# Walking the attention scores by head group instead of by query tile, with the last block's schedule moved 32 slots later

## What is computed

```
x = x + 0.5 * ffn(layernorm(x))          # "b" in the kernel
x = x + attention(layernorm(x))          # 16 heads of 16 features, top 31 of 512 keys kept
x = x + 0.5 * ffn(layernorm(x))          # "a" in the kernel

attention: Q, K, V = x W^T + b;  scores = Q K^T / 4
           thresh = 31st largest of each row of 512 scores; smaller ones become -inf
           softmax, times V, heads joined, times Wo^T + bo
ffn:       rw = softmax over 16 experts of gated cosine logits (at least 2 experts)
           q, k, v = sum over experts of rw * (h W_e);  causal attention over the 512 tokens, 64 wide
           output = sum over experts of rw * (attn o_proj_e)
```

## Time and profile before

| what | value |
|---|---|
| median of 3 runs | 4930.05 us (4927.84 to 4933.91) |
| the profiled execution | 4933.91 us, of which the span from first to last instruction is 4932.1 us |
| busy share of the span | DVE 92%, PE 82%, POOL 75%, ACT 69%, PEld 67% |
| mean granted TensorE clock | 0.915 of full speed |
| DMA | mean 47 GB/s, queue 1 busy 16.5% of 16 engines |

### The profile page before, as it was taken

The page is one execution under the profiler, slowest core; times in us unless marked ns, Lnnn a source line. Parts: engine busy times, 40 slices in busy tenths (PEclk is TensorE's granted clock), DMA queues, the critical chain, the costliest instruction groups (busy, mean ns, idle before and its releaser), DMA issues.

```text
span 4932.1 us, 111636 instructions
## 1 busy us (share of the span) xinstructions
PE 4021.6 (82%) x29004; PEld 3308.1 (67%) x29004; DVE 4550.9 (92%) x10838; ACT 3383.9 (69%) x8261; POOL 3711.1 (75%) x5070
## 2 busy tenths in 40 slices
PE   5767888888888888888888988888888888877667
PEld 4555766776777667676776767777677677765556
DVE  0199999999999999999999999999999999999990
ACT  2366777777777777777777777777777777766662
POOL 4456788878878787878878787888878788865554
PEclk8887999999999999999999999999999999998778
DMA  2201111111111111111111111111111111111011
GB/s 83 51 20 33 47 50 49 52 48 47 53 46 53 48 51 48 51 50 49 51 46 53 48 50 48 49 51 48 51 48 53 47 52 48 50 38 27 20 28 49
DMA packets 243181, 232.19 MB, mean 47 GB/s; under 512 B 27075, under 2 KB 176580, under 8 KB 242244
## 3 DMA queue, kind: packets, MB, share of 16 engines
q1 hardware_dynamic: 242500, 224.49, 16.5%
HBM read 214.98 MB, written 9.44 MB: 46 GB/s over the span
## 4 chain that ended last, share of the span: by engine, by line
issue 37%; POOL 30%; PE 17%; DVE 10%; ACT 3%; DVEq 1%; POOLq 1%; SPq 1%; ACTq 0%; DMA 0%
POOL HS L899 13%; DVE M L802 6%; PE pQ L490 6%; POOL S L940 6%; POOL mixT L917 4%; DVE W L804 3%; PE pFa L434 2%; PE pFa L438 2%; PE pST L474 1%; PE pST L507 1%; PE pFb L458 1%; PE pFa L378 1%; PE pO L531 1%; DVEq L240 1%; PE pFa L380 1%
## 5 line engine op out<-in xcount | busy, mean ns | idle before, releaser
L490 PE MATMUL pQ<-wf_sb,HS 128*128 128x192 f32 x8192 | 1679.8, 366 | 475.0 <-POOL HS L899 473.7
L802 DVE MAX8 M<-W 128x8 f32<-128x512 f32 x3072 | 1953.4, 675 | 0.0
L490 PEld LDWEIGHTS pQ<-wf_sb,HS 128*128 128x128 f32 x8192 | 1545.1, 216 | 556.5 <-POOL HS L899 431.3
L804 DVE MATCH_REPLACE8 W<-M,W 128x512 f32<-128x512 f32 x2048 | 1363.0, 670 | 0.0
L940 POOL TENSOR_TENSOR S<-S,RL 128x512 f32<-128x512 f32 x1024 | 1306.4, 1277 | 0.0
L706 ACT ACTIVATE RL<-S,NBI 128x512 f32<-128x512 f32 x1024 | 762.4, 745 | 388.9 <-POOL S L940 387.4
L935 POOL TENSOR_TENSOR NBI<-M,edge 128x4 f32<-128x4 f32 x512 | 102.1, 199 | 881.1 <-DVE M L802 850.7
L711 ACT ACTIVATE S<-S,NBI 128x512 f32<-128x512 f32 x1024 | 748.4, 731 | 2.1 <-POOL S L940 2.1
L695 ACT COPY S<-pST 128x512 f32<-128x512 f32 x1024 | 525.2, 600 | 242.7 <-PE pST L474 242.7
L804 DVE MATCH_REPLACE8 W<-M,S 128x512 f32<-128x512 f32 x1024 | 681.5, 670 | 0.0
L802 DVE MAX8 M<-S 128x8 f32<-128x512 f32 x1024 | 648.6, 672 | 29.5 <-issue 28.7
(11 more groups left out here) (219 smaller groups left out, 5477.9 us busy)
## 6 DMA issues: line engine op xcount, KB each, us to landing
RB<-rows_b SPq DMA_DIRECT2D x384, 256.0 KB, 3.2
RB<-rows_a SPq DMA_DIRECT2D x384, 256.0 KB, 3.3
x_b<-in_x SPq DMA_DIRECT2D x64, 128.0 KB, 2.8
out_y<-y SPq DMA_DIRECT2D x64, 128.0 KB, 1.7
wf_sb<-in_wf SPq DMA_DIRECT2D x1, 3072.0 KB, 10.4
wof_sb<-in_wof SPq DMA_DIRECT2D x1, 1024.0 KB, 12.4
rows_b<-rwT_b SPq DMA_DIRECT2D x64, 8.0 KB, 1.3
rows_a<-rwT_a SPq DMA_DIRECT2D x64, 8.0 KB, 1.3
```

What stands on the lines that cost most here:

```text
L490: mm = nc.tensor.matmul(pQ[:, 0:QKV], HS[:, k % 2, e, i, :], wf_sb[:, i, at:at + QKV], start=k + e + i == 0, stop=(k, e, i) == (3, 3, 1))
L802: nc.vector.max(m, src[i]).then_inc(s_tk, 1)
L804: nc.vector.match_replace(W[:, i, :], m, src[i], -BIG).then_inc(s_tk, 1)
```

## The change

The quads of a sequence are walked head group by head group: `g = c % QUADS // TPB`, `m = c % TPB`. A query tile's context is then complete only with the last head group: tile m's last `CTX` is at slot 69 + 4 m + 64 per sequence. So:

- chain "a" is due 32 slots later: the `- 2 * TILE` is gone, `ctx_rec` of tile t is at 69 + 16 t, `y` at 119 + 16 t. Its place in the period of 16 slots is the same.
- `ctxr` holds two whole sequences instead of two tiles; which half is used is a run-time slice inside the loop (`ds(bt % 2, 1)`) on ACT (CTX), DVE (`ctx_rec`) and POOL (`ctx_norm`). ACT no longer waits there for `ctx_norm`; its wait for `s_ot` is now followed by a semaphore increment (`held`).
- `RINGX` is 9.
- V: ACT copies heads 0 to 7 from PSUM straight into `V`, and only heads 8 to 15 through `Vst`; one `VMOVE` copy at slot 20 replaces four.
- PE's waits for K1 and for V are moved to the quads that first need them.

```diff
-RINGX = 7
+RINGX = 9
...
-    "a": {k: v - 2 * TILE for k, v in {
+    "a": {
         "ctx_rec": 69, "ctx_norm": 71, "ctxT": 72, "x": 74, "x_mean": 75, "x_sq": 76, "x_rstd": 77, "h": 78,
...
-    }.items()},
+    },
...
-VMOVE = 7
+VMOVE = 20
...
-        Vst = sb("Vst", P, TPB, D)
+        Vst = sb("Vst", P, TPB, P)
...
-        ctxr = sb("ctxr", P, 2, GROUPS, CTXW)
+        ctxr = sb("ctxr", P, 2, GROUPS, TPB * CTXW)
...
             def scores(n, c):
-                m, g = c % QUADS // GROUPS, c % GROUPS
+                g, m = c % QUADS // TPB, c % TPB
...
                 if at := due(w, j, SC, 4, QUADS * NB):
                     n, c = at
-                    if c % QUADS in (0, 2):
+                    if c % (QUADS // 2) == 0:
...
                 if at := due(w, j, PV, 4, QUADS * NB):
                     n, c = at
-                    g = c % GROUPS
-                    if c % QUADS < GROUPS:
-                        pe.wait_ge(s_vm, w.count(GROUPS, c // QUADS * GROUPS + g + 1))
+                    if c % QUADS == 0:
+                        pe.wait_ge(jobs["b"].sem["read"], fill("b", w, j + PROJ["V1"] - PV) + 1)
+                    if c % QUADS == QUADS // 2:
+                        pe.wait_ge(s_vm, w.count(1, c // QUADS + 1))
                     wait(pe, s_o, n)
                     pe.wait_ge(s_pe, w.count(SPAN, 4 * (c + 1)))
+                    g = c % QUADS // TPB
...
-                        nc.scalar.copy(Vst[:, 2 * c:2 * c + 2, :], F[:].rearrange("p (n m) -> p n m", n=2)
-                                       ).then_inc(q["read"], 1)
+                        two = F[:].rearrange("p (n c h d) -> p n c h d", n=2, c=2, h=H // 2)
+                        nc.scalar.copy(V[:, 2 * c:2 * c + 2, 0:H // 2, 0:HD], two[:, :, 0, :, :])
+                        nc.scalar.copy(Vst[:, 2 * c:2 * c + 2, :],
+                                       F[:].rearrange("p (n c m) -> p n c m", n=2, c=2)[:, :, 1, :]).then_inc(q["read"], 1)
...
                 if at := due(w, j, CTX, 4, QUADS * NB):
                     n, c = at
-                    g, m = c % GROUPS, c // GROUPS % 2
-                    if g == 0 and not (isinstance(n, int) and n < 2 * GROUPS):
-                        act.wait_ge(jobs["a"].sem["ctx_norm"], w.count(TPB, c // GROUPS - 1))
-                    act.wait_ge(s_ot, n + 1)
-                    nc.scalar.copy(ctxr[:, m, g, :].rearrange("p (h e) -> p h e", h=HG),
-                                   pO[:, P:2 * P].rearrange("p (h e) -> p h e", h=HG)[:, :, 0:HD + 1]).then_inc(s_o, 1)
-                for g in range(GROUPS):
-                    if due(w, j, VMOVE + 4 * g, SPAN, NB):
-                        nc.scalar.copy(V[:, :, HG * g:HG * (g + 1), 0:HD],
-                                       Vst[:, :, g * HG * HD:(g + 1) * HG * HD].rearrange("p n (h d) -> p n h d", h=HG)
-                                       ).then_inc(s_vm, 1)
+                    bt, g, m = w.count(1, c // QUADS), c % QUADS // TPB, c % TPB
+                    held(act, s_ot, n + 1)
+                    nc.scalar.copy(ctxr[:, ds(bt % 2, 1), g, m * CTXW:(m + 1) * CTXW].rearrange(
+                        "p a (h e) -> p (a h) e", h=HG),
+                        pO[:, P:2 * P].rearrange("p (h e) -> p h e", h=HG)[:, :, 0:HD + 1]).then_inc(s_o, 1)
+                if at := due(w, j, VMOVE, SPAN, NB):
+                    n, c = at
+                    nc.scalar.copy(V[:, :, H // 2:H, 0:HD], Vst[:].rearrange("p n (h d) -> p n h d", h=H // 2)
+                                   ).then_inc(s_vm, 1)
...
                 if at := tile(J, "ctx_rec", w, j):
                     t, c = at
-                    held(dve, s_o, GROUPS * t + GROUPS)
-                    nc.vector.reciprocal(crec[:], ctxr[:, c % 2, :, :].rearrange("p g (h e) -> p g h e", h=HG)[:, :, :, HD]
-                                         ).then_inc(q["ctx_rec"], 1)
+                    bt, m = w.count(1, c // TPB), c % TPB
+                    held(dve, s_o, w.count(QUADS, c // TPB * QUADS + QUADS - TPB + m + 1))
+                    nc.vector.reciprocal(crec[:], ctxr[:, ds(bt % 2, 1), :, m * CTXW:(m + 1) * CTXW].rearrange(
+                        "p a g (h e) -> p (a g) h e", h=HG)[:, :, :, HD]).then_inc(q["ctx_rec"], 1)
```

More of the change, by code:

```diff
@@ L838, in ffn @@
                     t, c = at
+                    bt, m = w.count(1, c // TPB), c % TPB
                     pool.wait_ge(q["ctx_rec"], t + 1)
-                    src = ctxr[:, c % 2, :, :].rearrange("p g (h e) -> p g h e", h=HG)
+                    src = ctxr[:, ds(bt % 2, 1), :, m * CTXW:(m + 1) * CTXW].rearrange("p a g (h e) -> p (a g) h e", h=HG)
                     nc.gpsimd.tensor_tensor(ctxn[:], src[:, :, :, 0:HD],
```

## The result

The changed kernel takes 4996.65 us (median of 4 runs, 4994.19 to 5000.2) against 4931.98 us for the kernel before: a ratio of 1.0134, 95% interval 1.0118 to 1.0148, so it is slower by 1.3%. The forecast was 4995 us. The profiled execution has a span of 4994.1 us, 62.0 us more than before.

A forecast was written before the change was run, and what follows sets the result against it. DVE was taken to bound only the middle, not the opening or tail. 64.2 - 1.4 + 2 = +64.8 us on the profiled 4933.9 gave 4998.7, or 4995 us against the median 4930.05; range 4980 to 5012 us.

The forecast's parts named there:

- Three stages, DVE binds only the middle: Whole execution: opening of 230 us, middle of 4567 us at DVE's pace, tail of 134.9 us without work for DVE.
- Two full periods, +64.2 us: Tail: seven copies of y instead of five behind the last score row, adding two full distances of 32.11 us.
- DVE work that leaves the middle, -1.4 us: Middle: two tiles' DVE steps of chain "a" fall behind the last TOP, about 0.7 us a tile.
- `ctx_rec` in `CTX`'s slot, +2 us: Middle, slot 5 of the next sequence: DVE waits for the CTX copy in 4 of 15 sequences, about 0.5 us each.
- Run-time slices, 0: Loop: computed addresses on ACT, DVE and POOL cost nothing; upper end 4.8 us on DVE.
- V and PE's waits, 0: V copies on ACT and PE's later waits for K1 and V: no cost or gain, as ACT is not the bound.
- The opening, unchanged: Before the first scores: the first MAX8 stays at 230 us.
- a first score row that isn't at 230: End of the opening: a first score row not at 230 us would show the forecast wrong.
- Rival 1: Middle: the new same-slot wait holds DVE in every sequence, 45 us rather than 2, about 5040 us; chance 0.06.
- rival 2: Tail: the two added periods go like the last tile alone, 22.45 us each, 4976 us; chance 0.06.
- rival 3: Tail: it is free, only DVE's 4567 us count and lose 1.4 us, 4929 us, no change; chance 0.02.
- Rival 4: Opening: relaxed waits for K1 and V bring the first scores earlier; a gain of 80 us gives 4915; chance 0.02.

The follow-up runs named there:

- e1: Kernel before, still tile by tile with static slices, but chain "a" 32 slots later (RINGX 9, ctxr four tiles deep): 4999.0 us, ratio 1.0138.
- e3: Changed kernel with all of chain "a" a further 16 slots later (RINGX 10): 5033.58 us, 36.9 above the changed kernel.
- e4: Changed kernel with ctx_rec at slot 67 instead of 69, so DVE waits once in each sequence: 5136.93 us, 140.3 above the changed kernel.
- e5: Changed kernel with V evicted as before, all through Vst and four moves at slots 7 to 19: 4997.7 us, ratio 1.0137.
- e2: Kernel before, tile by tile with static slices, but chain "a" 16 slots later (RINGX 8): 4966.98 us, 34.2 above the kernel before.
- e7: Kernel before with HS and mixT on DVE instead of POOL, chain "a"'s behind the last score row and chain "b"'s before slot 0: 4899.35 us, ratio 0.9938.
- e6: Kernel before with chain "a"'s HS and mixT computed by DVE instead of POOL behind the last score row: 4921.18 us, ratio 0.9984.

## Why the prediction was right, step by step

- **Three stages, DVE binds only the middle:** held. The middle is 4563 to 4566 us in all six kernels of the table, whatever the order of quads.
- **Two full periods, +64.2 us:** the tail grew by 66.4. The two added distances are 33.91 and 32.48 us rather than 32.11 twice; e1 gives the same from the old order, and e1 to e3 the price per tile (34.2, 32.0, 36.9). The growth is inside the stated bounds of 60.6 to 68.7. Why a full period varies from 31.9 to 35.3 us is not settled.
- **DVE work that leaves the middle, -1.4 us:** the middle is 1.9 shorter. It can't be told from the scatter of 3 us between the table's kernels. The term was a little small: 0.464 us is the mean of the reductions and not their upper end, and the MAX8 on `v_a` (0.15 us) was left out. The DVE records of chain "a" behind the last score row add up to 6.1 us instead of 3.5.
- **`ctx_rec` in `CTX`'s slot, +2 us:** mis-sized, it was 0 in the middle. No sequence waited there. Behind it stood a step that failed: I let PE's idle time ahead of the expert group grow, since tile 1's work is narrower than tile 3's. It shrank, in the sequence shown from 2.99 to 1.88 us, and in the 14 sequences with such a row it was 1.38 to 4.13 us, 11 of them under 2.4 (before: 1.54 to 3.66, 9 of them over 2.9). What shortened it I did not isolate. The reading that the idle time decides between a fast and a slow group fails too: before, groups behind 3.46 us were fast once and slow twice. The four groups of the changed kernel between 4.19 and 4.38 us and the one of 4.12 were shorter than the 5.33 to 5.39 of before, and the copy behind them was still 0.9 to 1.2 us ahead. That the copy is on time was measured; e4 shows that the price I named for the other case was real, and even low.
- **Run-time slices, 0:** held; 48 address computations of 64 ns (median) on DVE's queue, no idle time.
- **V and PE's waits, 0:** held (e5: 4997.7).
- **The opening, unchanged:** the profiled execution was 2.5 us earlier. e5 and the table show 225.19 to 232.04 for unchanged openings, so 2.5 us can't be told from scatter between executions. By the letter the prediction had named "a first score row that isn't at 230" as a sign of being wrong, and a last one at 4796 to 4800 us, where it is 4791.55. Both signs were drawn narrower than the scatter; the waits that the second was to show did not occur.
- **Rival 1** (45 us by waits in every sequence) fell with the trace and e3; **rival 2** (cheap periods of 22.45) with seven copies of `y`; **rival 3** (free by occupancy) with e1 and e2: DVE has the highest occupancy, and two kernels with the same DVE work (e1 and before) are 66 us apart. **Rival 4** fell with the table; e7 shows that the mechanism itself, an earlier first score row, is worth nearly its full length once something moves it (21.8 us of time for 23.4 us between e6 and e7).
- The rule that rival 3 names (the Trainium skill, "Perfetto Trace Analysis", section on the most-contended engine) takes the engine with the highest occupancy as the one to optimize first, and the same page allows that this engine changes over time. This trace agrees for the middle. In the tail the busiest engine is PE with 25.02 of 34 us, and no engine is full.

The tail's 66.4, the middle's -1.9 and the opening's -2.5 make the trace's 62.0. The timed medians are 64.7 apart; the two figures differ by less than the runs of either kernel among themselves (about 6 us). That the forecast of 4995 lies within 2 us of 4996.65 is in part luck: on the profiled executions the tail was 2.2 us more than forecast, the middle 2.5 and the opening 2.5 us less (62.0 against 64.8), and a full period varies by 3 us.

## What to carry to other kernels

In a software pipeline with one saturated engine, count which steps fall behind that engine's last instruction: a delay of the other steps was free before it and cost one full tail period per tile behind it. Price it by the distance between equal events in the tail that already exists, and take the distance with as many chains overlapping as the added ones will have. And look at the opening and the tail for the engine that is idle there: moving 24 products to it brought the first scores 21 us earlier. Which step to move is read from the chain of that stage: here it was `HS` in the opening and `mixT` in the tail.

## What was not expected of the hardware

- A product of 128 x 1024 f32 with two broadcast inputs took 2.35 us on POOL and 1.23 us on DVE (e6 expected about half).
- A wait of DVE in the middle makes the chain that it waits for slower too: PE went idle for 3.66 us, ran the next expert group at the lower of its two levels (5.29 instead of 2.83 us), and the wait became 9.38 us in that sequence, 8.3 on average, where 6.2 was worked out from the undisturbed trace. Where the group stayed fast the wait was 6.9.
- Speeding one engine up in a tail period left PE's first expert group slow, 5.06 to 5.46 us, and put a DMA on the chain that had been hidden; a full period gained 0 to 2 us of the 3 to 4 expected.
